# A transformer layer on one core: one group's transfers issued between two parts of a stack, and reciprocals half a slot earlier

## The reference

```
x = x + attention(layernorm(x))
x = x + (layernorm(x) @ W.T + b) + (layernorm(x) @ V_r) @ C.T

attention:  q, k, v = split(x @ qkv_w.T)          # 16 heads of 16 channels
            q, k    = rotary(q), rotary(k)
            s       = q @ k.T * SCALE + min(pos_k - pos_q, 0) * slope[head] * 8
            out     = softmax(s) @ v
            return out @ proj_w.T + proj_b
```

## Time and profile before

| | |
|---|---|
| median of 3 runs | 2248.63 us |
| the profiled execution: its time | 2251.11 us |
| its span, first to last instruction | 2249.8 us |
| granted TensorE clock, mean over the span | 0.976 |
| TensorE busy (matmuls) | 2138.2 us, 95% |
| VectorE busy | 1929.7 us, 86% |
| ScalarE busy | 1489.1 us, 66% |
| GpSimd busy | 1153.0 us, 51% |
| SyncE's queue, share of the 16 DMA engines' span | 32.9% |

### The profile page before, as it was taken

How to read it: one execution, slowest core, us unless ns; L and a number is a source line. 1 busy time by engine, 2 the same in 40 slices (tenths; PEclk the granted TensorE clock), 3 DMA queues, 4 the chain that set the end, 5 groups by cost and what they waited for, 6 DMA issues and landing times.

```text
span 2249.8 us, 77620 instructions
## 1 busy us (share of the span) xinstructions
PE 2138.2 (95%) x31524; PEld 1133.6 (50%) x31524; DVE 1929.7 (86%) x5690; ACT 1489.1 (66%) x2178; POOL 1153.0 (51%) x970
## 2 busy tenths in 40 slices
PE   3799999999999999999999999999999999999995
PEld 1245555555555555555555555555555555555553
DVE  4589888998889898888989898999989899999972
ACT  1167766677677666777766767776676677667662
POOL 4435455645455464545555554555555455555412
PEclk8599999999999999999999999999999999999997
DMA  4323333333333433333332333334234333333310
GB/s 120 93 75 107 98 96 109 94 91 106 109 88 110 115 94 91 106 107 90 107 115 77 104 113 90 107 106 113 76 105 115 80 114 108 97 89 107 107 32 25
DMA packets 158870, 218.50 MB, mean 97 GB/s; under 512 B 19024, under 2 KB 104912, under 8 KB 158512
## 3 DMA queue, kind: packets, MB, share of 16 engines
q1 hardware_dynamic: 157232, 211.44, 32.9%
q10 hardware_dynamic: 1280, 2.10, 0.3%
HBM read 36.52 MB, written 16.78 MB: 24 GB/s over the span
## 4 chain that ended last, share of the span: by engine, by line
PE 70%; SPq 8%; DVE 8%; DMA 5%; issue 4%; POOL 3%; ACT 1%; DVEq 0%; ACTq 0%; POOLq 0%
PE ps_s L368 22%; PE ps_o L389 16%; PE ps_misc L352 12%; PE ps_misc L339 8%; SPq L884 6%; DMA den<-o_sb 4%; DVE junk L533 4%; PE ps_t L376 4%; PE ps_misc L330 3%; PE ps_misc L408 3%; PE ps_misc L399 1%; POOL halves L859 1%; DVE ps_t L543 1%; DVE attn_t L559 1%; SPq L892 1%
## 5 line engine op out<-in xcount | busy, mean ns | idle before, releaser
L533 DVE CUSTOM_DVE_ANT_0 junk<-ps_s,alibi 128x512 bf16<-128x512 f32 x2048 | 1327.2, 684 | 206.9 <-PE ps_s L368 160.6
L678 ACT ACTIVATE pt<-ps_t 128x1024 f32<-128x1024 f32 x1024 | 1049.4, 1025 | 557.6 <-DVE ps_t L543 543.3
L368 PE MATMUL ps_s<-at 64*128 64x512 f32 x2048 | 817.5, 464 | 40.4 <-DVE row_max L533 32.3
L376 PE MATMUL ps_t<-at 64*128 64x512 f32 x2048 | 770.0, 452 | 1.8 <-ACT pt L678 1.7
L389 PE MATMUL ps_o<-pt,v_one 128*17 128x128 f32 x16384 | 641.6, 274 | 4.0 <-ACT pt L678 1.4
L389 PEld LDWEIGHTS ps_o<-pt,v_one 128*17 128x17 f32 x16384 | 431.0, 98 | 310.3 <-issue 211.3
L543 DVE SCALAR_TENSOR_TENSOR ps_t<-diag,slope,ps_t 128x256 f32<-128x256 f32 x1024 | 488.1, 477 | 13.3 <-PE ps_t L376 13.3
L368 PEld LDWEIGHTS ps_s<-at 64*128 64x128 f32 x2048 | 331.2, 187 | 311.2 <-DVE row_max L533 250.1
L837 POOL TENSOR_TENSOR rope_b<-raw,rope_sin 128x512 f32<-128x512 f32 x128 | 164.3, 1283 | 494.4 <-ACT raw L728 489.1
L376 PEld LDWEIGHTS ps_t<-at 64*128 64x128 f32 x2048 | 323.4, 185 | 40.2 <-ACT pt L678 33.0
L853 POOL TENSOR_TENSOR rope_a<-rope_a,swapped 128x512 f32<-128x512 f32 x128 | 161.8, 1285 | 350.4 <-DMA swapped<-rope_b 350.4
(11 more groups left out here) (79 smaller groups left out, 1570.5 us busy)
## 6 DMA issues: line engine op xcount, KB each, us to landing
at<-halves SPq DMA_DIRECT2D x192, 512.0 KB, 4.9
swapped<-rope_b SPq DMA_DIRECT2D x256, 128.0 KB, 2.5
x_in<-in_L_attn_x_dram SPq DMA_DIRECT2D x32, 512.0 KB, 4.4
num<-o_sb SPq DMA_DIRECT2D x512, 32.0 KB, 2.0
x_res<-in_L_attn_x_dram SPq DMA_DIRECT2D x32, 512.0 KB, 4.3
out_dram<-x_hat SPq DMA_DIRECT2D x32, 512.0 KB, 5.4
at<-spread_den SPq DMA_DIRECT2D x60, 64.0 KB
at<-max_t ACTq DMA_DIRECT2D x128, 16.0 KB
```

The source lines that it names most:

```text
L368: pe.matmul(ps_s[:, t % 2, :], operand(n, 0)[:, t * P:(t + 1) * P], operand(n, 1), start=True, stop=True).then_inc(s_done, 1)
L376: pe.matmul(ps_t[:, j, :], operand(n, 1)[:, j * P:(j + 1) * P], operand(n, 0), start=True, stop=True).then_inc(t_done, 1)
L533: dve.tensor_tensor_reduce(junk[:, t % 2, :], ps_s[:, t % 2, :], alibi[:, off:off + N], 1.0, LOWEST, ALU.add, ALU.max, row_max[:, hb % 2, ...
L678: act.activation(pt[:, h % 2, 2 * pair:2 * pair + 2, :], ps_t[:, 2 * pair:2 * pair + 2, :], ACT.Exp).then_inc(exp_done, 1)
```

## The change

In SyncE's program the stack is split: its first transfer stays at slot 8 hb - 5, its other two, with their wait for `low_done`, go to slot 8 hb - 4. Within a slot the outputs of a group stand ahead of the stack, so that the group of slots 4 and 12 is now issued between the first transfer and the other two. In VectorE's program the two reciprocals move up by half a slot: the first, with its wait for `den_placed`, to the second half of slot 13 (offset 29), the second to the first half of slot 14. The number of instructions, transfers and bytes stays.

```diff
@@ VectorE, in the loop over the halves of a slot
-                    b = batch_at(slot, 30)
-                    if b is not None:
-                        denominators(b, half)
+                    for part in range(2):
+                        b = batch_at(slot, (29, 30)[part])
+                        if b is not None and half == 1 - part:
+                            denominators(b, part)
@@ SyncE
                     sp.wait_ge(high_done, 2 * hb + 2)
                     stack(hb, 0, 0, 0)
+                hb = half_at(slot, -4)
+                if hb is not None:
                     sp.wait_ge(low_done, 2 * hb + 2)
                     stack(hb, 1, 1, 0)
                     stack(hb, 2, 0, 1)
```

## The result

The changed kernel takes 2216.68 us, median of 4 runs (2214.39 to 2218.82), against 2247.85 us for the kernel before in the same comparison (4 runs). The ratio is 0.9862, 95% interval 0.9845 to 0.988: 31 us or 1.4% faster. The profiled execution took 2215.47 us with a span of 2214.2 us and a mean granted clock of 0.978; that of before took 2251.11 us.

What follows compares the result with a forecast made beforehand. VectorE's wait for the denominators was taken as the stall between TensorE and VectorE in step; 37.0 + 5.2 - 5.6 = 36.6 us off 2251.1 gives 2214.5, less 2.5 profile offset, 2212 us, range 2203 to 2232.

Steps and rivals of the forecast that it cites:

- What bounds the kernel: VectorE's first reciprocal waits for the denominators behind SyncE's stack transfers: 28 waits, 39.8 us in all, 1.42 us each.
- What a wait costs: Each reciprocal wait costs its length less 0.10 us that VectorE makes up: 37.0 us over 28 waits.
- The dips: Lowered TensorE clock behind some waits: four stretches at 1.31 us each, 5.2 us, would go with the waits.
- The landing: Denominators land right behind the first stack transfer, about 1112.1 and 1176.2 us in the two batches read.
- The new waits: Remaining reciprocal waits for the denominators at the new place: mean 0.2 us, 5.6 us over 28 batches.
- rival B: First stack transfer or held issue lands denominators 0.6 us later in all 28 batches: 17 us more, 2229 us; chance 0.12.
- The held issue: SyncE's issue of the denominators held 4.00 us, to 1109.64, as the second stack transfer's was; the upper-end reading.
- rival D: Issue held to 1109.64, denominators land 4.08 us on; wait grows from 1.09 to 2.0 us, 2274 us; chance 0.06.
- The stacks behind: SyncE's two later stack transfers still land before TensorE needs them, 0.8 us left at worst, some 3 likely: cost 0.
- The signs: Profile checks: reciprocal waits under 12 us, not 44; clock 1.00; denominators issued about 2.3 us after first stack transfer; others.
- The sum: Whole kernel: 37.0 + 5.2 - 5.6 = 36.6 us saved, 2214.5 us profiled, 2212 us given for the runs.

Runs made afterwards that it cites:

- SyncE's order alone: From the changed kernel, the reciprocals put back at slot 14, keeping SyncE's split stack: 2211.7 us, ratio 0.9837.
- zeros last: From the changed kernel, the two transfers of zeros and their wait moved behind the stack's third transfer: 2208.7 us, ratio 0.9828.
- zeros moved alone: From the kernel before, only the zeros moved behind the last group's numerators, the stack in one piece ahead of the denominators: 2212.53 us, ratio 0.9826.
- second profile: Profile of the changed kernel run again without an edit, as yardstick: 2217.92 us, ratio 0.9867.

## Why the prediction was right, point by point

The time lay within the range, the median 5 us above the figure given, and the mechanism was the forecast one: the denominators land behind the first stack transfer in place of the third, and the wait goes. The size of what is left of the wait came out near by luck, as told below.

**What bounds the kernel** held. The wait of 1.4 us a batch was real stall: with it gone in three ways (SyncE's order alone, zeros last, zeros moved alone) slots 32 to 480 come to 1807.3, 1807.5 and 1807.7 us, 41.5 to 41.9 below the kernel before. The prediction had 42.2 for what can go.

**What a wait costs** held, batch by batch. Take the time of each batch, from the row maximum that opens slot 8 to the same one a batch later, and compare it with the median of the three kernels without the wait. In the kernel before, 24 batches are longer by their wait less 0.09 to 0.15 us (the prediction had 0.10).

**The dips** held. The four batches with a dip are longer by a further 1.3 to 1.4 us each (1.31 predicted). The dips went with the waits, and came back in greater number where the waits grew.

**The landing** held, and the raises of the semaphores in the traces show why. The two transfers of zeros and the denominators have 4 rows or 4 partitions. The Trainium skill (DMA: Bandwidth & Descriptors, Why a DMA increments its semaphore by 16 and not by 1) states that a transfer whose slowest dimension is 4 uses the lowest 4 engines. The trace agrees with the number: the denominators' semaphore is raised five times for each transfer, once 0.4 to 0.6 us after its issue ends and then four times more, where a stack transfer raises its own 16 times. Which four engines these are isn't shown. The raises for batch 14:

| transfer | issued | raises of its semaphore |
|---|---|---|
| changed kernel, first stack transfer | 1085.88 | twelve from 1089.96 to 1091.41, then 1094.06, 1094.90, 1095.10, 1095.22 |
| changed kernel, denominators | 1087.77 | 1093.16, then 1094.24, 1095.08, 1095.28, 1095.39 |
| zeros last, first stack transfer | 1080.99 | sixteen from 1084.75 to 1085.10 |
| zeros last, denominators | 1083.02 | 1084.03, then four from 1085.04 to 1085.20 |

With the zeros ahead, twelve shares of the stack transfer land together and four come late, and each of the denominators' four follows one of these by 0.17 to 0.18 us. So it is in all 28 batches (median 0.18 us, the last one 0.17 to 0.74 behind). With the zeros last the gap between the twelfth and the thirteenth raise is 0.3 us at most. By size, 128 KB of zeros on four engines put 32 KB on each, as much as the 512 KB of a stack transfer put on each of sixteen. That is an estimate from the transfers' sizes. The experiments say the same from outside: taking away the zeros, 128 KB, speeds the first stack transfer by 4.2 us in one batch and 3.9 in the mean, while taking away 384 KB of the store, spread over 128 rows, speeds it by 0.7 and 0.4.

The prediction also weighed 0.8 to 2 us to landing for a small transfer, from the Trainium skill (DMA: Bandwidth & Descriptors, Latency and other measured facts), where the 0.8 is stated for a round trip to HBM. From issue to the last raise the denominators took 6.6 to 8.8 us in the changed kernel and 2.2 to 3.7 with the zeros last.

**The new waits** were sized at 0.2 us a batch and 5.6 us in cost. Measured 10.3 us of waits, 0.37 a batch, and 1812.1 - 1807.3 = 4.8 us of cost in the first profile; 13.1 us of waits and 1814.8 - 1807.3 = 7.5 us in the second. Three errors met here, and that the cost was right to 1 or 2 us is luck. First, the size came from two batches: the same reading of the landing rows gives some 2 us of waits in sum for all 28 batches, not 5.6. Second, "the first stack transfer lands whatever stands behind it" is off: it landed 9.0 us after its issue in the mean, where before it was 8.3, and in the very two batches of the prediction 9.3 in place of 8.6 and 10.1 in place of 7.8. These two batches waited 1.15 and 1.30 us, where 0.4 and 0 were predicted. That is rival B's mechanism, a landing later than read; why the transfer takes longer with the new order isn't shown. Third, a wait at the new place costs less than its length less 0.10. Batch by batch, waits up to 0.3 us cost nothing (22 batches with waits up to 0.34 us cost 0.1 us in sum), and the six longer ones cost their length less 0.25 to 0.29. In the rows above one sees where that comes from: the half behind the second reciprocal has no reciprocal and no division in it, and its idle time before the next row maximum shrank from some 0.39 us to 0.24 behind the wait of 1.15. That is a gain of the new place that the prediction put at 0, and it made the small waits free.

**The held issue**, half of rival D, came true (3.86 us; 4.2 in the mean of 28 batches), and the denominators did not land later for it: in batch 14 the issue was held until 1087.77 + 4.97 = 1092.74, and the landing at 1095.39 still came 0.17 us behind the first stack transfer's. The two times run together and aren't added. What holds the issue at that moment isn't shown; that it needs the zeros is, because with them last it took 0.59 us.

**The stacks behind** held: the last landed at 1030.72 + 5.7 = 1036.4, 1.9 us ahead of the first product that wants it, at 1038.34, against 0.8 in the worst reading and some 3 in the likely one. Over 28 batches the change has used up 3.8 us of that margin, from 6.7 to 2.9 us in the mean, and 1.8 is the least. One detail failed at no cost: `o_copied` was said to be up in time for the last group, and SyncE waited for it in 11 of 28 batches.

**The signs** held but for one: the waits of the reciprocal were to sum to under 12 us in place of 44, the last batch included. They sum to 14.5, and to 17.3 in the second profile. The denominators' issue stood 2.45 us behind the first stack transfer's, as said.

**The sum**: 36.6 us predicted, 37.1 in the steady stretch, 35.6 between the two profiled executions. The step that was off is the last one, the level. I took the profiled execution as 2.5 us above the runs and the changed kernel to keep that distance; it lay 1.2 us below its own median instead, and the medians are 31 us apart, 2212 predicted against 2216.7. That offset rested on a single execution of the kernel before. In two profiles of the changed kernel the start and the end of the program agree (402.1 and 401.9 us) and the waits differ (10.3 and 13.1 us), so that the waits are one part of the scatter. The runs without a profile have no trace that could divide the rest.

## What to carry to other kernels

Before moving a small transfer forward in a queue, ask what holds the issue: here a pair of transfers to 4 rows, 128 KB in all, kept the whole queue back for 4 us, and moving them behind the numerators was worth as much as the reordering (ratio 0.9826 against 0.9837), with the denominators left behind the whole stack. A consumer should be moved earlier only by what is left of the landing's gain once the old wait is paid. Here the denominators came 1.42 + 2.10 - 0.37 = 3.15 us sooner in the mean; 1.42 of that went into the old wait, and the reciprocal was moved by 2.10 where 1.73 were left. SyncE's order alone beats the full change by 6 us. The versions without the wait (SyncE's order alone 0.9837, zeros last 0.9828, zeros moved alone 0.9826) can't be told apart. A reading from two batches out of 28 can be far off the mean, so read the landing in all of them. And a wait costs its length only when the next stage has no idle time to give it back; count the idle time of the halves behind it.

## What the runs showed of the hardware that was not expected

A transfer to 4 rows delays the transfers behind it on four DMA engines alone: behind 128 KB of zeros, twelve shares of a 512 KB transfer landed 4.1 to 5.5 us after its issue and the last four 8.2 to 9.3 us after it, and with the zeros issued behind it all sixteen landed 3.8 to 4.1 us after it (batch 14). An 8 KB transfer from 4 partitions landed 0.18 us behind these last four.

Another queue is no way around it: with the zeros ahead the same 8 KB took 6.3 to 10.0 us to land from ScalarE's queue and 6.6 to 8.8 us from SyncE's in the changed kernel, against 2.2 to 3.7 us from SyncE's with the zeros last. An issue from ScalarE's queue costs that engine 0.60 us, and with its wait the next activation started 0.68 us later, 0.45 us of the kernel's time a batch.

The issue of 8 KB was held for 3.86 us by transfers that had been issued some 4 us before it, and took 0.59 us where they weren't there.

Behind waits of 2.3 to 5.0 us stood stretches of 4 us with a granted clock of 0.50 to 0.74, so partly or wholly at 1.2 GHz. In the kernel before, TensorE had stood still 1.5 to 1.8 us in one piece ahead of each. But the longest wait of that kernel, 2.9 us with TensorE still for 2.1, was followed by none, nor were four of the 28 waits with the reciprocals alone moved (2.8 to 3.1 us), nor any wait of the changed kernel, up to 1.5 us.
